# Expert tokens of three of four jobs loaded five tiles at a time, with every engine's order written anew

## The reference, cut to what matters

```python
h = jax.nn.relu(flat_x @ W1[e] + b1[e])
y = h @ W2[e] + b2[e]
final_output = final_output + y * w[:, None]
```

## Time and profile before

| | |
|---|---|
| median of 3 runs | 587.65 us (585.57 to 588.38) |
| the profiled execution, its own time | 592.57 us |
| its span, first to last instruction | 590.4 us |
| granted TensorE clock, mean | 0.884 of full speed |
| busy: TensorE, VectorE, ScalarE, GpSimd | 465.2, 302.5, 247.6, 170.3 us |
| token loads (`slot_x`), 64 KB each | 60 |
| weight loads, 514 KB each | 60 |

### The profile page before, as it was taken

How to read it: one execution, slowest core, us unless ns; L and a number is a source line. 1 busy time by engine, 2 the same in 40 slices (tenths; PEclk the granted TensorE clock), 3 DMA queues, 4 the chain that set the end, 5 groups by cost and what they waited for, 6 DMA issues and landing times.

```text
span 590.4 us, 11797 instructions
## 1 busy us (share of the span) xinstructions
PE 465.2 (79%) x4233; PEld 368.1 (62%) x4233; DVE 302.5 (51%) x767; ACT 247.6 (42%) x711; POOL 170.3 (29%) x210
## 2 busy tenths in 40 slices
PE   3897789995999998325799587786899988677895
PEld 2786678782789876022788576564677835465442
DVE  4657695657654520262123132848523616978674
ACT  3343566443565663011244224433466615253222
POOL 5043152136413100627200500635311050133210
PEclk9897899995899999555899989869899969799888
DMA  7987550000134444603499777102164110000000
GB/s 248 331 219 150 167 137 32 1 2 32 33 99 121 128 120 141 246 15 110 119 291 282 217 207 219 37 1 68 36 174 119 29 41 10 0 6 2 0 6 13
DMA packets 50630, 62.12 MB, mean 105 GB/s; under 512 B 6704, under 2 KB 39664, under 8 KB 50320
## 3 DMA queue, kind: packets, MB, share of 16 engines
q1 hardware_dynamic: 48048, 56.88, 33.3%
q0 software_dynamic: 2048, 4.20, 2.4%
q10 hardware_dynamic: 480, 0.32, 0.2%
HBM read 52.86 MB, written 16.94 MB: 118 GB/s over the span
## 4 chain that ended last, share of the span: by engine, by line
PE 52%; DVE 13%; issue 10%; ACT 6%; another core or an unknown queue 2%; POOL 2%; DMA 1%; SPq 0%; POOLq 0%; DVEq 0%; ACTq 0%
PE PS L881 7%; PE PS L871 5%; PE PS L1466 4%; PE PS L855 4%; PE PS L1434 3%; PE PS L867 3%; PE PS L1861 3%; PE PS L1713 2%; PE PS L1265 2%; DVE arena L1762 2%; PE PS L1251 2%; PE PS L1448 2%; PE PS L847 1%; PE PS L1692 1%
## 5 line engine op out<-in xcount | busy, mean ns | idle before, releaser
L795 POOL DMA_INDIRECT picked<-slots_y,place_u x32 | 30.9, 964 | 54.4 <-DMA slots_y<-slot_y 45.7
L1434 PE MATMUL PS<-featT,rot_wqk 128*128 128x128 f32 x256 | 34.1, 286 | 2.5 <-ACT rot_yT L1536 1.4
L881 PE MATMUL PS<-expert_w,hid 128*128 128x128 f32 x204 | 30.7, 293 | 5.1 <-ACT slot_y L963 2.3
L1434 PEld LDWEIGHTS PS<-featT,rot_wqk 128*128 128x128 f32 x256 | 32.1, 202 | 3.2 <-issue 3.0
L881 PEld LDWEIGHTS PS<-expert_w,hid 128*128 128x128 f32 x204 | 26.9, 202 | 8.8 <-issue 5.7
L937 ACT ACTIVATE slot_xT<-PS 128x128 f32<-128x128 f32 x60 | 16.6, 279 | 35.9 <-PE PS L847 28.1
L1395 POOL TENSOR_TENSOR rot_sh<-rot_sh,const 128x512 f32<-128x512 f32 x16 | 21.3, 1334 | 34.4 <-DVE rot_sh L1566 34.4
L1466 PE MATMUL PS<-rot_W,rot_yT 128*128 128x128 f32 x256 | 30.1, 276 | 0.9 <-ACT rot_yT L1536 0.9
L1466 PEld LDWEIGHTS PS<-rot_W,rot_yT 128*128 128x128 f32 x256 | 29.2, 192 | 1.2 <-ACT rot_yT L1536 1.1
L1202 POOL TENSOR_SCALAR cond_st<-cond_st 128x1 f32<-128x1 f32 x16 | 3.1, 196 | 92.1 <-ACT cond_zn L1310 91.9
L847 PE MATMUL PS<-const,slot_x 128*128 128x128 f32 x60 | 17.6, 298 | 14.1 <-remote 8.0
(11 more groups left out here) (322 smaller groups left out, 1213.2 us busy)
## 6 DMA issues: line engine op xcount, KB each, us to landing
expert_w<-packed SPq DMA_DIRECT2D x30, 514.0 KB, 4.1
rot_qk<-packed SPq DMA_DIRECT2D x15, 514.0 KB, 4.6
slot_x<-slots_x SPq DMA_DIRECT2D x60, 64.0 KB
slots_y<-slot_y SPq DMA_DIRECT2D x60, 64.0 KB
packed<-in_moe_w_dram SPq DMA_DIRECT2D x6, 512.0 KB
packed<-in_moe_w_dram SPq DMA_DIRECT2D x3, 1024.0 KB
rot_yT<-packed SPq DMA_DIRECT2D x5, 514.0 KB, 5.1
rot_W<-packed SPq DMA_DIRECT2D x5, 514.0 KB
```

The lines of the kernel that those rows point to most:

```text
L795: nc.gpsimd.indirect_dma_start(picked[:, j, n, :], None, ys[half], bass.IndirectOffsetOnAxis(place_u[job % 2][:, j, n:n + 1], 0)).then_inc ...
L881: mm = nc.tensor.matmul(full(bank_of(MO_, i), 2 * P, 3 * P), hid[:, i % 2, c, :], weights(i)[:, lo + E * (c - first):lo + E * (c - first) ...
L1434: mm = nc.tensor.matmul(full(RB + part, P * c, P * c + P), wr[:, part, c, :], featT[:, P * n:P * n + P], start=True, stop=True)
```

## The change

Tokens of job 0 are loaded as before. Those of jobs 1 to 3 are loaded by nine transfers of five units each (`m_load_group`, 320 KB), into four places that lie behind the weight buffers in the tiles of the `rot` attention; a group waits for its job's scatter, and for the end of `rot` or for the transposes of the five units that had its place. `tokens_of` gives the transpose its tile and its semaphore. The squares before the router of layer 1 stay one ScalarE instruction for each tile, and the four jobs keep their order. The whole table `TIMES` is another one: on every engine most steps have moved. Of it, the diff shows the rows of the loads alone.

```diff
@@ -116,203 +116,201 @@
...
-    "m_load_slots": (135.47, 135.94, 136.41, 136.88, 140.46, 141.52, 148.94, 154.45, 160.73, 163.18, 174.49, 178.25, 179.27, 183.93, 186.55, 257.28,
...
+    "m_load_slots": (140.13, 140.6, 141.07, 141.54, 143.6, 144.44, 154.57, 159.3, 163.18, 166.24, 175.53, 185.35, 186.31, 191.97, 195.02),
...
+    "m_load_group": (262.12, 262.61, 263.1, 271, 278.24, 286.8, 384.48, 384.97, 385.46),
...
@@ -474,6 +472,9 @@
         flat = [qk[:].rearrange("p s k c t -> p (s k c t)"), yT[:].rearrange("p h b t -> p (h b t)"), rW[:].rearrange("p h e -> p (h e)"), wr[:].rearrange("p k c t -> p (k c t)")]
         W += [flat[m][:, (NW + FF0 // P) * c:(NW + FF0 // P) * (c + 1)] for m, c in ((0, 0), (0, 1), (0, 2), (1, 0), (2, 0), (3, 0))]
         WBIAS = [w[:, NW:NW + FF0 // P] for w in W]
+
+        XG = 5
+        group_x = [f[:, at:at + XG * E].rearrange("p (s e) -> p s e", e=E) for f, at in zip(flat, (3 * (NW + FF0 // P),) + (NW + FF0 // P,) * 3)]
         wqk_in = qk[:, 1].rearrange("p k c t -> p (k c t)")
         wv_in = acc[:].rearrange("p n e -> p (n e)")
         wo_in = yT[:].rearrange("p h b t -> p (h b t)")[:, 0:AH * AD].rearrange("p (c e) -> p c e", e=E)
@@ -731,6 +732,13 @@
         def weights_there(i):
             b, uses, _ = buffer_of(i)
             return w_loaded[b], 16 * uses
+
+        def tokens_of(i):
+
+            if i < SLOTS:
+                return slot_x[i % XB][:], (x_loaded[i % XB], 16 * (i // XB + 1))
+            g, s = divmod(i - SLOTS, XG)
+            return group_x[g % XB][:, s, :], (x_loaded[g % XB], 16 * (len(range(g % XB, SLOTS, XB)) + g // XB + 1))
 
         def half_b_ready(i):
 
@@ -755,18 +763,28 @@
                 sp.dma_start(W[b][:], here.rearrange("o p f -> p (o f)")).then_inc(w_loaded[b], 16)
 
             def load_slots(i):
-                job, half, layer, s = job_of(i)
-                sp.wait_ge(scattered[job % 2], 16 * 2 * HT * (job // 2 + 1))
+
+                sp.wait_ge(scattered[0], 16 * 2 * HT)
                 if i >= XB:
                     sp.wait_ge(m_xT_ps, i - XB + 1)
-                sp.dma_start(slot_x[i % XB][:], xs[half][P * s:P * s + P, :]).then_inc(x_loaded[i % XB], 16)
+                sp.dma_start(slot_x[i % XB][:], xs[0][P * i:P * i + P, :]).then_inc(x_loaded[i % XB], 16)
+
+            def load_group(g):
+
+                job, half, layer, s = job_of(SLOTS + XG * g)
+                sp.wait_ge(scattered[job % 2], 16 * 2 * HT * (job // 2 + 1))
+                if g < XB:
+                    sp.wait_ge(f_ready, TILES)
+                else:
+                    sp.wait_ge(m_xT_ps, SLOTS + XG * (g - XB + 1))
+                sp.dma_start(group_x[g % XB], xs[half][P * s:P * (s + XG), :].rearrange("(s p) e -> p s e", p=P)).then_inc(x_loaded[g % XB], 16)
 
             def store_slots(i):
                 job, half, layer, s = job_of(i)
                 sp.wait_ge(m_y_ready, i + 1)
                 sp.dma_start(ys[half][P * s:P * s + P, :], slot_y[i % YB][:]).then_inc(m_stored[i % YB], 16)
 
-            return [("m_load_weights", load_weights), ("m_load_slots", load_slots), ("m_store_slots", store_slots)]
+            return [("m_load_weights", load_weights), ("m_load_slots", load_slots), ("m_load_group", load_group), ("m_store_slots", store_slots)]
 
         def mixture_pool(pool):
             def scatter(i):
@@ -839,12 +857,13 @@
                 nc.tensor.matmul(full(MM_[job]), gateT[:], last_b[job % 2][:], start=True, stop=True).then_inc(biasing, 1)
 
             def transpose_slots(i):
-                pe.wait_ge(x_loaded[i % XB], 16 * (i // XB + 1))
+                tokens, there = tokens_of(i)
+                pe.wait_ge(*there)
                 if i >= 2:
                     pe.wait_ge(m_a_ps, i - 1)
                     pe.wait_ge(m_b_ps, i - 1)
                 claim(pe, (bank_of(MT_, i),), (m_xT_ready, i + 1))
-                nc.tensor.transpose(full(bank_of(MT_, i), 3 * P, 4 * P), slot_x[i % XB][:], k["ident"]).then_inc(m_xT_ps, 1)
+                nc.tensor.transpose(full(bank_of(MT_, i), 3 * P, 4 * P), tokens, k["ident"]).then_inc(m_xT_ps, 1)
 
             def hidden_a(i):
                 job, half, layer, s = job_of(i)
```

255 lines of the change are left out of this document (127 added, 128 removed), and 126 rows, old and new, of the table TIMES.

## The result

On the first chips measured the changed kernel took 588.31 us (median of 20 runs, 576.79 to 594.62), the kernel before 590.70 us (20 runs, 585.57 to 598.73). The ratio is **0.9871, with an interval of 0.9826 to 0.9916**. It compares only the undisturbed runs, those within 1.5% of a kernel's fastest, which are six of the changed kernel's 20; the mean of all runs, which I use beside it from here on, went from 591.4 to 587.5 us: 3.9 ± 2.5 us less, 0.65%. Either way the change is faster, by less than 2%, and the forecast was no change, +1.4 us. That the forecast time, 589.0 us, lies 0.7 from the measured median is luck: it was added to 587.65, the median of three runs, and twenty runs of the same kernel have 590.70.

The account below looks back on a forecast made before the run. The prediction took TensorE (52% of the chain of waits) and the seams between jobs as the bounds; its terms, 2.4 + 0 − 3.3 + 2.1 − 0.5 + 0.7, gave +1.4 on 587.65, so 589.0 us, range 582.5 to 598.0.

Parts of the forecast that it names:

- a): Ahead of job 0's counting: four tap matmuls come, one `r_scores` leaves; +2.4 us, between 0 and +4.4.
- e): End of job 2: earlier gates save up to 2.8 us, two more GpSimd spreads cost up to 1.3; −0.5 us.
- b): Job 0's units: `rot` steps moving in (+4.67 us) and out to behind the last unit (−4.68) cancel; net 0.
- sign of being wrong outright: Start of job 1 shifting by over 5 us would mean orders matter in a way the sums miss.
- second rival: Job 0's last units and combine transposes held behind `rot`'s last steps: +4.7 us, sum +6.1, 593.8 us; chance 0.35.
- Ahead of the units: Between job 0's counting and first unit: fewer `rot` steps, claimed free at a low clock; 0 us.
- c): Gather of job 0 no longer waits for taps after the last store; −3.3 us, gain between 2.0 and 4.7.
- d): Start of job 1: TensorE waits for a 320 KB group instead of a 64 KB load; +2.1 us, high end +6.3.
- SyncE's new wait: Fourth group load waits for job 2's scatter, with a weight load and job 1's first stores queued behind; put at 0.
- f): End part: `f_gate` and `f_quantise_y` stand ahead of other tiles' work; +0.7 us, between 0 and +2.9.
- first rival: Seams between jobs: free taps, quick gather, interpolated group load, early gates all come out well; −5.1 us, 582.6 us; chance 0.20.
- third rival: Stalls put down to another core or unknown queue shrink with fewer small DMAs; −10.4 us, 577.2 us; chance 0.05.

Follow-up runs that it names:

- e5: Kernel before with only the taps (and two folds they force) moved ahead of job 0's counting; 7.0 ± 2.6 us slower than before, ratio 1.0125, second kind.
- e8: Changed kernel with job 0's last unit put ahead of `rot`; 5.1 ± 5.1 us faster than before, ratio 0.9788, second kind of chip.
- e9: Changed kernel with e8's move, plus the tail of `rot`'s last tile behind the first routing; 6.0 ± 3.1 us slower than before, ratio 1.0141, first kind.
- e6: Before's order to job 0's stores with taps ahead of the counting, then changed order and groups; 4.1 ± 2.6 us slower than before, ratio 1.0039, second kind.
- e15: Before's order to job 0's stores, changed order behind, groups, last two taps behind job 0's gather; +0.7 ± 3.2 us against before, ratio 0.9981.
- e4: Changed table throughout, but 45 single loads instead of groups; −1.5 ± 2.2 us against before, ratio 0.9982, first kind of chip.
- e1: Kernel before with only the loads replaced by the nine groups; +2.1 ± 2.9 us against before, ratio 1.0007, first kind of chip.
- e3: Before's table to the end of job 0's stores, changed table from there on, groups; −4.4 ± 4.3 us against before, ratio 0.9878, first kind.
- e12: The same kernel as e3, run again on the first kind of chip; −1.6 ± 2.0 us against before, ratio 0.9985.
- e13: Changed kernel with one `log` projection put back between job 3's routing and counting; 8.3 ± 3.1 us faster than before, ratio 0.9825, second kind.
- e14: Kernel before with that one `log` projection moved away from between job 3's routing and counting; 3.9 ± 2.0 us slower than before, ratio 1.0051, second kind.

## Why the prediction was wrong, point by point

The sum said +1.4. By the table, on the first kind the early part is +1.6 and the late part −3.9 (9.0 of the scatter itself is equal), −2.4 in all; the two measurements of the changed kernel there, weighted by their runs, are −2.9. Two terms failed: a), "I take +2.4, since the chain in that stretch is full of single TensorE items", where the stretch with the taps came out +0.3 longer, and e), "I take −0.5", which was −2.4. b), "The net is 0", failed the other way, with +3.0, and hid part of it. And five stretches that the prediction gave nothing (ahead of job 0's units, job 1's units, the way to job 3's scatter, that to job 3's units and these) moved by +2.5, −3.2, −2.1, +0.9 and +1.9: on the first kind of chip they cancel, on the second the first of them is −3.1, and the gain there is the early part's. The prediction's own sign of being wrong outright, a start of job 1 shifted by over 5 us, came true there: −6.4 by the table.

- **a) The taps, +2.4: too large.** From the second tile's logits to the counting, where all four taps stand, it is +0.3 us in every trace. Three of the taps are in the chain there with 0.86 each, 2.6 in all, so their price was right; but an `r_scores` of 2.0, counted, and three folded products of 0.89 each of the `log` attention (L1678), not counted, left that stretch, and an `r_times_x` of 1.1 came. The counting as a whole came 1.4 us earlier on the first kind and 4.0 on the second. That difference arises ahead of the second tile's logits, and is within the spread of traces of the same order, 8 us (−2.9 ± 2.5 over 18 traces), so its cause stays open. e5 shows what the place can cost: alone, in before's order, the same move cost 7.4 us. I priced a move in the old neighbourhood, when the neighbours moved too.
- **b) Job 0's units, 0: wrong, and the second rival half right.** +3.0 and +3.5 us, and they lie in the last unit: from its transpose to the last store 10.65 us in place of 6.72, as `r_scores` and `r_output` now stand ahead of its output (rows above). That is the rival's first half. Its second half, transposes of the combine held by `r_output` of the last tile (6.6 us at half clock and not 3.57), happened too, but cost little: in the profile the first transpose came 3.9 us behind its sums, and the last sum 13.7 us behind the first gather in place of 12.2; in the seven other traces of this order but e8 and e9 it is 12.2 to 12.8. The rival's price was +4.7 for the whole. It was outweighed, not refuted.
- Ahead of the units: predicted free ("so those steps were free"). It is −3.1 on the second kind, and on the first +2.5, for the burst. The `r_scores` that a) counted as gone went here (L1467 at 137.31, 4.23 us at half clock), and no term has it.
- **c) The gather, −3.3: right.** −2.7 and −2.3. With the taps alone away the gather comes 5.1 to 5.6 us behind the store (e5, e6, e15), in the changed order 4.2; whether the weight loads behind the store make that difference wasn't tested.
- **d) The first group, +2.1: right in kind, a little large.** +1.6 in the two profiles, +1.5 by the table. The group took 2.88 us, under my interpolation of 3.3. The Trainium skill's page "DMA: Bandwidth & Descriptors", section "Anatomy of one DMA — SWDGE (gpsimd) path", whose fit gives an estimate of 2.75 us for 320 KB, was closer for the group, and not for the 64 KB load, where 1.61 was measured against 2.15. On the first kind it was also covered, by the wait behind job 2's scatter. SyncE's new wait showed no cost.
- **Job 1's units, not predicted:** −3.2. About 1.2 is the first pair of units (8.1 us from first to third transpose in place of 9.3, the cover just named), 1.5 by the means of the table's traces. Another 1.1, 0.8 by the means, is order: in the changed kernel each transpose stands between two units' outputs (transpose, output, transpose, hidden products), and the third and fourth pair, at full clock, take 4.1 us each, where before they took 5.0 and 4.3. e4, with single loads and the same order, has 4.1 and 4.1 there; e1, with groups and the old order, 5.0 and 4.3. The rest, about 0.9, is in the second pair and goes with TensorE's granted clock there: 4.4 us at 1.00 (e3, e12), 5.7 to 5.9 at 0.72 (changed, before), 6.6 at 0.58 (e4).
- **e) The end of job 2, −0.5: too small.** Job 2 ends 1.7 us shorter and the gather is 0.7 sooner. Then the way to job 3's scatter is 2.1 shorter. TensorE in order of time around routing and counting of job 3, kernel before:

```profile
391.10 1.88 PE L898 MATMUL PS<-feat,xT_half 128*128 128x8 f32 x8
392.83 3.76 PE L1713 MATMUL PS<-log_W,arena 128*128 128x128 f32 x16
396.38 3.00 PE L1692 MATMUL PS<-uT,log_M 128*128 128x128 f32 x16
399.21 0.18 PE L817 MATMUL PS<-picks,before_b 128*128 128x32 bf16 x1
```

The changed kernel:

```profile
387.84 3.76 PE L1711 MATMUL PS<-uT,log_M 128*128 128x128 f32 x16 [0.67 <-ACT arena L1768]
391.39 0.37 PE L909 MATMUL PS<-const,xres 128*128 128x128 f32 x1
...
392.69 0.95 PE L917 MATMUL PS<-feat,xT_half 128*128 128x8 f32 x8
...
394.39 2.02 PE L1732 MATMUL PS<-log_W,arena 128*128 128x128 f32 x16 [0.17 <-ACT arena L1752]
...
397.35 0.19 PE L835 MATMUL PS<-picks,before_b 128*128 128x32 bf16 x1
```

Before, two products of the `log` attention (3.76 and 3.00 us) stood between the routing (L898) and the counting (L817), 8.1 us apart in start. In the changed kernel one of them (L1711) stands ahead of the last transpose, and routing and counting (L917, L835) are 4.7 us apart. The other took 2.02 us in place of 3.76, at a granted clock of 1.00 in place of 0.50. e13 and e14 show that the step matters at this place (+2.1 put back, in the trace), but not that it gains alone.
- Job 3: +0.9 on the way to its units and +1.9 in them; not predicted. In its units TensorE does the same steps in both profiles (517 records each), so it is the order; which step costs it isn't settled.
- **f) The end, +0.7:** within the noise, −0.5 with all behind job 3.

The first rival, faster by the seams (−5.1), is nearest to what was measured, in part by luck: nearly free taps and early gates are in it, but not the longer last unit of job 0, nor the unpriced stretches. The third rival (stalls that go with fewer transfers) was wrong: the share was 2 and 3% in two traces before and is 3% after. But the stalls are real, and on the second kind of chip, where no chain has them, the kernel before takes 19 to 20 us less; how much of that the stalls make isn't shown.

## What to carry to other kernels

When a change rewrites an order, price each stretch between two landmarks that both orders pass with the same set of steps, all of them, and not only the places where the diff is easy to read: five stretches that got no price here moved by 0.9 to 3.2 us each, as much as any that had one. Joining the two orders at such a landmark is the experiment that says which part gains; a single step moved alone mostly moved a wait. And measure on more than one chip before a difference of 1% is explained.
